# Attention of the expert stage in a two-layer tower: in nine of eighteen steps TensorE does values, then maxima, then scores

## The reference, cut to what matters

```python
sx = einsum('bsh,ndh->bnsd', x, hl_w) + hl_b[None, :, None, :]
q = einsum('bnsd,neod->bneso', sx, wq)
k = einsum('bnsd,nod->bnso', sx, wk)
v = einsum('bnsd,nod->bnso', sx, wv)
scores = einsum('bnesd,bntd->bnest', q, k) * d ** 0.5 + causal
att = softmax(scores, axis=-1)
qkv = einsum('bnest,bntd->bnesd', att, v)
```

## Time and profile before

| | |
|---|---|
| median of three runs | 6436.79 us (6429.37 to 6442.04) |
| profiled execution | 6439.12 us, its span 6437.4 us |
| expert stage (first to last V) | about 4022 to 5938 us of the span |
| busy over the span | PE 5476.4 us (85%), DVE 4516.4 (70%), ACT 3123.9 (49%), POOL 1481.8 (23%) |
| granted TensorE clock, mean | 0.874 |

### The profile page before, as it was taken

One profiled execution on the slowest core, in us unless ns is written; L12 is line 12 of the kernel. 1 busy time (PEld: TensorE's weight loads), 2 busy tenths in 40 slices (PEclk: granted clock), 3 DMA queues, 4 the chain that ended last, 5 costly groups with the idle time before them and its releaser, 6 DMA issues. The chain is left out here.

```text
span 6437.4 us, 128358 instructions
## 1 busy us (share of the span) xinstructions
PE 5476.4 (85%) x44752; PEld 2403.9 (37%) x44752; DVE 4516.4 (70%) x8593; ACT 3123.9 (49%) x3314; POOL 1481.8 (23%) x1329
## 2 busy tenths in 40 slices
PE   2777777779999999999999995999999999998545
PEld 1444444442222222222322222444444444444222
DVE  3655565656676767676767675888888888887666
ACT  0111111115555555555555551777777777777111
POOL 1000000000000000010000004655655655655000
PEclk9666666669999999999999995999999999999555
DMA  0000000000000000000000000000000000000000
GB/s 13 1 1 1 1 1 0 0 0 1 2 1 2 1 2 1 2 1 2 1 2 1 1 1 1 2 3 3 2 3 3 2 3 3 2 3 2 7 10 10
DMA packets 30275, 15.50 MB, mean 2 GB/s; under 512 B 29060, under 2 KB 29127, under 8 KB 29608
## 3 DMA queue, kind: packets, MB, share of 16 engines
q1 hardware_dynamic: 26208, 6.09, 0.5%
q10 hardware_dynamic: 3400, 0.95, 0.1%
HBM read 2.29 MB, written 4.19 MB: 1 GB/s over the span
## 5 line engine op out<-in xcount | busy, mean ns | idle before, releaser
L1906 DVE TENSOR_REDUCE f_mp<-psum 128x1 f32<-128x512 f32 (+2 forms) x2614 | 1344.2, 574 | 236.8 <-PE psum L1754 184.5
L1122 ACT ACTIVATE a_prob<-psum,escale 128x1024 f32<-128x1024 f32 x1024 | 1139.8, 1113 | 615.3 <-PE psum L1195 606.8
L1704 ACT ACTIVATE f_prob<-psum,escale_f 128x1024 f32<-128x1024 f32 x1152 | 1242.5, 1112 | 280.0 <-PE psum L1822 151.5
L1203 PE MATMUL psum<-a_prob,a_v 128*64 128x512 f32 x4096 | 1102.6, 617 | 0.0
L1267 DVE TENSOR_REDUCE a_mp<-psum 128x1 f32<-128x512 f32 x1035 | 715.6, 691 | 517.7 <-PE psum L1150 498.7
L1744 PE MATMUL psum<-f_kf,f_qf 64*128 64x512 f16 (+3 forms) x3138 | 677.5, 333 | 51.3 <-DVE f_mp L1906 43.9
L1269 DVE TENSOR_REDUCE a_mp<-psum 128x1 f32<-128x512 f32 x1035 | 703.7, 680 | 0.0
L1073 POOL TENSOR_TENSOR h<-h,a_u 128x512 f32 x129 | 163.6, 1268 | 2205.6 <-DVE a_u L1283 2205.6
L1589 POOL TENSOR_SCALAR f_hi<-f_raw,part 128x512 f16<-128x512 f32 x330 | 516.7, 1566 | 477.4 <-ACT f_raw L1671 477.4
L1835 PE MATMUL psum<-f_prob,f_vh 128*32 128x512 f32 (+3 forms) x6144 | 614.7, 495 | 2.8
L1814 PE MATMUL psum<-f_qf,f_kf 64*128 64x512 f16 (+3 forms) x3074 | 511.5, 329 | 28.9 <-issue 14.7
(11 more groups left out here) (393 smaller groups left out, 8213.7 us busy)
## 6 DMA issues: line engine op xcount, KB each, us to landing
out_dram<-h SPq DMA_DIRECT2D x16, 256.0 KB, 2.6
f_qf<-f_rowT SPq DMA_DIRECT2D x130, 4.0 KB, 2.1
ids<-in_itok_BS_dram SPq DMA_DIRECT2D x80, 4.0 KB
wd<-in_L_ffn_Wd_dram SPq DMA_DIRECT2D x1, 256.0 KB
wd<-in_L_ffn_Wd_dram ACTq DMA_DIRECT2D x1, 256.0 KB
mgate<-in_L_ffn_gate_w_dram SPq DMA_DIRECT2D x16, 0.2 KB
ids<-in_x_dram SPq DMA_DIRECT2D x16, 4.0 KB
aw<-in_L_attn_WQ_dram ACTq DMA_DIRECT2D x1, 128.0 KB
```

The lines of the kernel that those rows point to most:

```text
L1122: act.activation(prob[:, kt % NPB], k.psum[:, 2 * (kt % 2):2 * (kt % 2) + 2].rearrange("p b n -> p (b n)"), ACT.Exp, scale=k.escale[:]).th ...
L1203: last = pe.matmul(ps[A_SUM][half * C:(half + 1) * C], lhsT=v[:, bp, kt, 0], rhs=prob[:, kt % NPB, half * HALF:(half + 1) * HALF], start=( ...
L1704: act.activation(prob[:, u % NPF], k.psum[:, pair:pair + 2], ACT.Exp, scale=k.escale_f[:])\
L1906: ins = dve.tensor_reduce(side[:, at:at + 1], bank_of(j + r)[:, col:col + nk], X, ALU.max)
```

## The change

Nine entries of the hand-written order, those with a V, all become V, then M, then S. Nothing else differs; every step still has the same letters.

```diff
-F_ORDER = ('SM', '0S1', '0S1', 'MSV', 'SM', 'SM', 'SMV', 'MS', 'SMV', 'MS', 'MSV', 'MSV', 'MS', 'SMV', '01S', 'SMV', 'MSV', 'SMV')
+F_ORDER = ('SM', '0S1', '0S1', 'VMS', 'SM', 'SM', 'VMS', 'MS', 'VMS', 'MS', 'VMS', 'VMS', 'MS', 'VMS', '01S', 'VMS', 'VMS', 'VMS')
```

## The result

The median is 6830.68 us (6821.69 to 6835.08, four runs) against 6434.09 us of the kernel before beside it: a ratio of 1.0613, 95% interval 1.0595 to 1.0632, 397 us slower. The profiled execution took 6828.58 us, its span 6826.9 us, 389 more than the one before.

A forecast was written before the change was run, and what follows sets the result against it. PE was taken as the bound, 96% busy in the expert stage. Nine intervals lose 7.0 us a group, 6.65 after v products; times 64 groups 426, less 10 at loop ends, 416: 6850 us, range 6670 to 6960.

The forecast's parts named there:

- V15 to V16: Time on PE from step 15's values product to step 16's, in one group: 3.1 us forecast, 1.88 before.
- The bare exponential: Steps 16 and 17: values product waits for the exponential of scores just made, costing PE 1.44 us each.
- The vector chain: Step 3's values product waits for f_oc behind four DVE readouts; 6.8 us after step 17's, now 5.62.
- The smaller waits: Waits between values products of steps 3 to 15, taken at full value; steps 3 to 6: 5.9 us, now 5.23.
- The rival that DVE and ACT, rested, would cover them: Only exponentials 16 and 17 count, other waits may go: 6555 to 6620 us, 6740 with half of them; chance 0.22.
- the walk: Sum of nine intervals between values products along PE in one group: 36.1 us against 29.16, 7.0 lost.
- the two deductions: Groups with a v product, one in four, lose 1.3 us less; eight loop ends take 10 us off in all.
- The clock rival: Clock also falls once a group: 6900 to 6955 us, above 7000 if low for most of the stage; chance 0.16.
- Faster: Values first gives DVE time before each maxima product, removing 40.4 us idle ahead of L1744: 6399 us; chance 0.02.

## Why the prediction was right

The forecast was 6850 with 6670 to 6960; 6831 was measured. Its own steps, against the group shown above (expected, then measured): V15 to V16 3.1, 2.98; V16 to V17 3.24, 3.25; V17 to V3 6.8, 6.51; V3 to V6 5.9, 5.89; V6 to V8 3.9, 3.80; V8 to V10 3.6, 3.55; V10 to V11 2.6, 2.39; V11 to V13 3.2, 3.05; V13 to V15 3.8, 3.73. The sum was 36.1 and is 35.15. So the mechanism held interval by interval, and not only in the sum.

*The bare exponential.* I gave 1.44 us from the slot behind the last mask product. Those start at 4109.06 and 4112.22, 0.06 later the slots would have begun, and V16 and V17 come at 4110.48 and 4113.73: 1.36 and 1.45, of which PE's idle rows show 1.21 and 1.29. That it is the place of V that lays them bare is shown by steps 16 and 17 alone, by the change without them, and by the sum taken one step later.

*The vector chain.* f_oc is what V3 waits for: 96.2 us ahead of L1835 in the stage, against the 60 to 100 foretold for both f_oc waits. Mis-sized by 0.3, most of it because four readouts take 4.8 us, not 5.0. The key product of even groups does not vanish in the chain, as I had it: V17 to V3 is 7.09 in front of those groups and 6.52 elsewhere. It was 6.20 and 5.63 before, so this cost the forecast nothing.

*The smaller waits.* Each came at the place named: 0.36 ahead of the output product for exponential 4 (I had 0.65 bare and 0.55 for M4, which took 0.88, so that the sum of V3 to V6 came out by errors that cancel), 0.41 ahead of V8 for the second f_oc, 0.68 ahead of S9 for the query product, 0.51 inside M12, 0.32 ahead of M14. The rival that DVE and ACT, rested, would cover them is out: the six middle steps alone cost 134 us.

*The average over groups.* 6.65 us was taken for a group, less 0.16 for the loop ends. From the first V15 to the last, the mean distance between groups went from 30.04 to 36.23, 6.19 us more. That the two lie so near owes something to luck. The two groups compared above are not of one kind: the one before is the last of a loop's eight (V13 to V15 3.12, in most others 2.94), the one after is not (3.73; the last of eight has 3.91). Of one kind, the walk's 36.1 stands against 35.33, 0.8 too much.

Against that, the two deductions hardly came. A group with a v product lost 0.56 us between V11 and V15 (from 7.46 to 8.02), where the ones beside it lost 1.03: 0.5 less, not 1.3, and the groups x = 0 and 4, which have no x, s or v product, lost some 0.4 more than the one that I walked. And V17 to V3 across a loop end went from 10.33 to 11.39, 1.06 more, where I had taken it to lose 1.25 less than elsewhere (0.89). So the walk was 0.8 us a group too long, the deductions were 0.5 too large, and 0.3 a group, 19 us, is left.

*The clock.* Rows of one loop end in the changed kernel, the columns as above:

```profile
4291.40:4295.00 3.60, 1.26 (x16) 0.47 (x16) 1.59 (x3) 1.81 (x3) 2.45 (x4) 1.00 0.04 11
4295.00:4298.40 3.40, 2.17 (x14) 1.04 (x16) 0.94 (x2) 2.17 (x2) 0.00 (x0) 0.54 0.02 7
4298.40:4301.80 3.40, 3.22 (x25) 1.56 (x23) 2.23 (x4) 2.03 (x2) 0.83 (x1) 0.50 0.01 2
```

The clock is at 0.5 (1.2 GHz) for 6.8 us where it was for 3.4. This is so at the seven loop ends inside the stage (the eighth closes it), and nowhere else in it is the clock low. It goes with the order of steps 16 and 17, whose idle times ahead of V16 and V17 lie right in front of the loop's pause of 3.05 us. With only these two steps changed it is 6.8 us at all seven (the first two rows below are of one), and with the change but for these two it is 3.4 at all seven (the last two rows). It is no strict rule: with the six middle steps alone changed it is 3.4 five times, 6.8 once, and once the clock does not fall.

```profile
4271.00:4274.40 3.40, 2.54 (x16) 1.15 (x18) 1.31 (x3) 1.77 (x2) 0.00 (x0) 0.50 0.03 7
4274.40:4277.80 3.40, 3.22 (x25) 1.55 (x23) 1.86 (x3) 2.06 (x3) 1.20 (x1) 0.50 0.01 2
...
4281.60:4285.00 3.40, 2.77 (x18) 1.27 (x20) 1.55 (x3) 1.75 (x2) 0.00 (x0) 0.50 0.03 7
4285.00:4288.40 3.40, 2.40 (x38) 1.33 (x34) 2.17 (x5) 2.85 (x3) 1.44 (x1) 0.99 0.01 2
```

Its price is small. V17 to V3 across a loop end is 4.30 us longer than in front of the other even groups in the changed kernel (11.39, 7.09) and 3.89 longer with steps 16 and 17 put back (10.09, 6.20); by estimate that is 0.4 us seven times, 3 of the 397 us. The clock rival as I had put it, a fall in every group, is out: over the group shown above the granted clock stayed at 1.00, through two idle times of 1.2 and 1.3 us with 2.0 us of work between:

```profile
4107.00:4145.00 38.00, 30.21 (x385) 14.29 (x380) 27.44 (x56) 25.12 (x26) 17.54 (x15) 1.00 0.01 2
```

The rule of the Trainium skill that I had weighed ("TensorE: Matmul & The Clock Gate", "A second HAM failure mode: psum-queue depth-cycling") does not show within the groups of this kernel.

*Faster* was out by the one point it hung on: exponentials 16 and 17 are not done when PE comes to them.

## What to carry to other kernels

Where engines look one item ahead of each other, the order of one engine's work decides how much of the others' latency shows. For each wait, ask how much of its own work the engine has between making the producer's input and needing its output; what it lacks to the producer's time plus the hand-over (here 1.11 us for an exponential, plus 0.34 and 0.05) it stands idle. When comparing two orders by intervals between marks, write down which work lies inside each interval in each order, or a part is counted in neither or twice.

## What the runs showed that I had not expected

The place of a 0.2 to 0.4 us maxima product is worth as much as that of the scores: with the scores first in both, 6725 with maxima last and 6463 with maxima second. The two costs are not separate: put together in the change, they come to 367 us against that run, not to the 551 of their sum. Between steps it is otherwise. The losses of three disjoint sets of steps added up to 381 of 397 us in a kernel in which three engines wait for one another in a ring; the prediction had given a chance of 0.22 to the smaller waits being hidden.
